# Groups taken from both ends of an image, and three weight chunks loaded ahead, in a two-layer metaformer kernel

## The reference

```python
x = x + deform_conv(ln(x))                      # layer 0: deformable 3x3 convolution
t = tokens(x)                                   # a pixel is a token of 128 numbers
t = t + top2_of_8_experts(ln(t))                # softmax router, 2 of 8 experts per token
x = image(t)
x = x + real(ifft2(mix(fft2(ln(x)))))           # layer 1: spectral mixing by alphas, betas
t = tokens(x)
t = t + top8_tokens_of_64_experts(ln(t))        # each expert takes its best 8 tokens of an image
x = image(t)
```

## Time and profile before

| | us |
|---|---|
| median of 3 runs (4090.9 to 4093.28) | 4091.42 |
| the profiled execution | 4085.3 |
| its span on the core | 4083.4 |
| busy: PE, DVE, ACT, POOL | 3799.8, 2587.2, 1809.6, 1597.7 |
| mean granted TensorE clock, share of full | 0.958 |

### The profile page before, as it was taken

The page is one execution under the profiler, slowest core; times in us unless marked ns, Lnnn a source line. Parts: engine busy times, 40 slices in busy tenths (PEclk is TensorE's granted clock), DMA queues, the critical chain, the costliest instruction groups (busy, mean ns, idle before and its releaser), DMA issues. The chain is left out here.

```text
span 4083.4 us, 88599 instructions
## 1 busy us (share of the span) xinstructions
PE 3799.8 (93%) x31447; PEld 2475.3 (61%) x31447; DVE 2587.2 (63%) x8511; ACT 1809.6 (44%) x4685; POOL 1597.7 (39%) x2857
## 2 busy tenths in 40 slices
PE   7999999999999999999968999999999999986458
PEld 5666666666666666666644445665666656654245
DVE  4444444444444444444428888999999999976633
ACT  4555555555555555555511112444444444456124
POOL 5454544555454544545412222323333233344210
PEclk9999999999999999999979999999999999989755
DMA  5454454554554545444426667777777777744879
GB/s 118 93 100 93 90 93 94 99 94 90 93 94 99 95 89 92 90 91 91 77 68 255 251 250 272 264 278 270 269 271 265 279 262 277 260 154 127 335 275 396
DMA packets 611531, 709.81 MB, mean 174 GB/s; under 512 B 62112, under 2 KB 494112, under 8 KB 594704
## 3 DMA queue, kind: packets, MB, share of 16 engines
q1 hardware_dynamic: 505616, 630.17, 53.7%
q10 hardware_dynamic: 104448, 71.85, 5.8%
q0 software_dynamic: 1024, 2.10, 0.1%
HBM read 521.20 MB, written 181.63 MB: 172 GB/s over the span
## 5 line engine op out<-in xcount | busy, mean ns | idle before, releaser
L362 PE MATMUL a_ob<-a_sr,wcv 128*128 128x512 f32 (+3 forms) x2820 | 1082.1, 518 | 0.8 <-DVE a_xo L492 0.8
L432 ACT COPY a_sr<-a_sb 128x576 f32<-128x576 f32 (+7 forms) x1296 | 621.9, 562 | 900.5 <-PE a_sb L347 892.9
L347 PEld LDWEIGHTS a_sb<-a_tt,a_win 32*128 32x128 f32 x19008 | 659.2, 186 | 258.4 <-issue 242.8
L347 PE MATMUL a_sb<-a_tt,a_win 32*128 32x144 f32 x19008 | 752.2, 301 | 12.8 <-ACT a_sr L432 11.5
L517 POOL TENSOR_TENSOR a_sx<-a_hh 128x576 f32<-128x576 f32 x260 | 378.3, 1455 | 925.5 <-DVE a_hh L469 917.4
L362 PEld LDWEIGHTS a_ob<-a_sr,wcv 128*128 128x128 f32 x2820 | 491.6, 191 | 279.0 <-issue 231.2
L1087 DVE TENSOR_TENSOR b_P<-b_P,b_x 128x1024 f32<-128x1024 f32 x512 | 620.3, 1212 | 0.0
L469 DVE TENSOR_SCALAR a_hh<-a_hh 128x576 f32<-128x576 f32 (+1 forms) x128 | 59.5, 465 | 839.2 <-ACT a_hh L411 839.2
L1217 POOL TENSOR_TENSOR b_ss<-b_st 128x12 f32<-128x12 f32 (+2 forms) x167 | 35.5, 213 | 1094.0 <-DVE b_pp L1162 957.5
L990 PE MATMUL b_z<-b_P,b_ew 128*128 128x512 f32 x1024 | 461.2, 593 | 0.0
L993 PE MATMUL b_z<-b_P,b_ew 128*128 128x512 f32 x1024 | 460.3, 592 | 0.0
(11 more groups left out here) (182 smaller groups left out, 5283.3 us busy)
## 6 DMA issues: line engine op xcount, KB each, us to landing
b_P<-pd SPq DMA_DIRECT2D x128, 2048.0 KB, 7.5
a_win<-xtp SPq DMA_DIRECT2D x2144, 36.0 KB
a_xin<-in_x SPq DMA_DIRECT2D x128, 256.0 KB, 6.0
xtp<-a_tn ACTq DMA_DIRECT2D x128, 256.0 KB, 2.3
x1d<-a_xo SPq DMA_DIRECT2D x128, 256.0 KB, 5.6
b_x<-x1d SPq DMA_DIRECT2D x128, 256.0 KB, 7.4
x2d<-b_xa SPq DMA_DIRECT2D x128, 256.0 KB, 2.7
d_wb<-in_w SPq DMA_DIRECT2D x16, 2048.0 KB, 18.6
```

The lines of the kernel that those rows point to most:

```text
L347: t = e.matmul(d[:, 0:3 * m_, :, NU_ * i:NU_ * i + NU_], win[32 * q:32 * q + 32, half_of(Q, j) % NWH, NWIN // 3 * h + i, :], m, start=(j = ...
L362: t = e.matmul(ob[:, r:r + m, :], k["wcv"][:, 3 * (2 - kr) + kx, :], rows[:, :, t_, :], start=(t_ == 0 and r == 0), stop=(t_ == 8))
L432: a = e.copy(bass.AP(d.tensor, d.offset, [list(d.ap[0]), [1152, ni], [1536, nk], [32, 4], [1, m]]), bass.AP(v.tensor, v.offset, [list(v.ap ...
```

## The change

Three things change.

1. **The order of groups.** Step n of the b half takes group `group_b(n)`: 0, 31, 1, 30, 2, 29, ... within each image. Step n of the c half takes `group_c(n)`: 31, 0, 30, 1, ..., at each step the mirror image of what the b half took at step n. So the c half of step n needs only step n's own mirrored group, and neighbours of `x2d` that were stored at steps n-1 and n+1. `LAG` falls from 39 to 11 and the ring `b_xf` from 35 units to 10. The list ends 28 slots earlier.
2. **The bias matmul** of the expert sum, with the wait for `b_pb`, comes after the eight expert matmuls instead of before them.
3. **Weights ahead.** The memory freed holds a tile `pw` of three chunks, which lives on into phase DE. In slots 118 to 129 SP issues one quarter of a chunk (512 KB) per slot, at the end of the slot. The ring of weights now has 8 slots, 3 in `pw` and 5 in `d_wb`; phase DE issues chunks 3 to 15. The buffers `e_x` and `e_o` lie in `pw`, whose last use by weights is long over when they are first filled.

```diff
-LAG = GI + 7
-XU = 3
-NU = GI + XU
+LAG = 11
+NU = 10
...
+NCH, EC, NW, AHEAD = 8, 8, 8, 3
+def chunk_part(pw, ins, i, part):
+    m, c = CHUNKS[i]
+    n = EC // 4
+    t = pw[:, i * 4096 + part * 1024:i * 4096 + part * 1024 + 1024].rearrange("p (e h) -> p e h", e=n)
+    return t, chunk_source(ins, m, c * EC + part * n, n)
...
 def order_b():
...
+        if 0 <= s - NG + 10 < 4 * AHEAD:
+            out.append(("ahead", s - NG + 10))
...
+def group_b(n):
+    b, i = divmod(n, GI)
+    return b * GI + (GI - 1 - i // 2 if i % 2 else i // 2)
+def group_c(n):
+    b, i = divmod(n, GI)
+    return b * GI + (i // 2 if i % 2 else GI - 1 - i // 2)
+def place_b(g):
+    b, h = divmod(g, GI)
+    return b * GI + (2 * h if h < GI // 2 else 2 * (GI - 1 - h) + 1)
...
             elif stage == "experts":
...
-                w.wait_ge(pb_in[G % NPC], 16 * (G // NPC + 1))
-                e.matmul(ZE[u][:, :, :], ebm[:, :], pb[:, G % NPC, :], start=True, stop=False)
                 for x in range(4):
-                    e.matmul(ZE[u][:, :, :], ew[:, x, :], P[:, G % NPB, :, x, :], start=False, stop=False)
+                    e.matmul(ZE[u][:, :, :], ew[:, x, :], P[:, G % NPB, :, x, :], start=(x == 0), stop=False)
             elif stage == "experts2":
                 for x in range(4, 8):
-                    t = e.matmul(ZE[u][:, :, :], ew[:, x, :], P[:, G % NPB, :, x, :], start=False, stop=(x == 7))
-                t.then_inc(mixed, 1)
+                    e.matmul(ZE[u][:, :, :], ew[:, x, :], P[:, G % NPB, :, x, :], start=False, stop=False)
+                w.wait_ge(pb_in[G % NPC], 16 * (G // NPC + 1))
+                e.matmul(ZE[u][:, :, :], ebm[:, :], pb[:, G % NPC, :], start=False, stop=True).then_inc(mixed, 1)
...
             elif stage == "fourier":
-                w.wait_ge(placed, G // GI * GI + GI)
+                w.wait_ge(placed, G + 1)
...
             elif stage == "load2":
-                g = G + 1 if G % GI < GI - 1 else G + 1 - GI
-                w.wait_ge(x2_out[G % 3], 16 * (G // 3 + 1))
-                w.wait_ge(x2_out[g % 3], 16 * (g // 3 + 1))
+                g = group_c(G)
+                for n in (place_b(g), place_b(g + 1 if g % GI < GI - 1 else g + 1 - GI)):
+                    w.wait_ge(x2_out[n % 3], 16 * (n // 3 + 1))
...
+            elif stage == "ahead":
+                dst, src = chunk_part(k["pw"], ins, G // 4, G % 4)
+                e.dma_start(dst, src).then_inc(k["w_in"][G // 4], 16)
...
-    wb = S("d_wb", [128, NW, 4096])
+    wb = S("d_wb", [128, NW - AHEAD, 4096])
...
-        for i, (m, c) in enumerate(chunks):
+        for i in range(AHEAD, len(CHUNKS)):
+            m, c = CHUNKS[i]
             if i >= NW:
-                used, last = chunks[i - NW]
+                used, last = CHUNKS[i - NW]
                 w.wait_ge(hidden if used == 1 else project, 2 * last + 2)
```

More of the change, by code:

```diff
@@ L844, with chunk_view, chunk_source @@
 NS = NG + LAG
+NCH, EC, NW, AHEAD = 8, 8, 8, 3
+CHUNKS = [(1, 0)]
+for _c in range(1, NCH):
+    CHUNKS += [(1, _c), (2, _c - 1)]
+CHUNKS.append((2, NCH - 1))
+def chunk_view(t, m):
+    return t.rearrange("p (e h) -> p e h", e=EC) if m == 1 else t.rearrange("p (e c o) -> p e c o", e=EC, c=4)
+def chunk_source(ins, m, e0, n):
+    if m == 1:
+        return ins["w1"][e0:e0 + n, 0:128, :].rearrange("e d h -> d e h")
+    return ins["w2"][e0:e0 + n, 0:512, :].rearrange("e (p c) o -> p e (c o)", c=4)
+def chunk_part(pw, ins, i, part):
[3 more added lines that the diff above has]
+    return t, chunk_source(ins, m, c * EC + part * n, n)
 def order_b():
@@ L853, in order_b @@
                 out.append((stage, s - lag))
-    return out
[L857 to L867, removed]
+        if 0 <= s - NG + 10 < 4 * AHEAD:
+            out.append(("ahead", s - NG + 10))
+    return out
+def group_b(n):
[7 more added lines that the diff above has]
+    return b * GI + (2 * h if h < GI // 2 else 2 * (GI - 1 - h) + 1)
 def image_rows(d, G):
-    return d[G * 512:G * 512 + 512, :].rearrange("(r w) c -> w r c", w=128)
+    g = group_b(G)
+    return d[g * 512:g * 512 + 512, :].rearrange("(r w) c -> w r c", w=128)
 def shifted_rows(G):
-    h = G % GI
+    h = group_c(G) % GI
     if h < GI - 1:
@@ L1001, in tensor @@
             elif stage == "fourier":
-                w.wait_ge(placed, G // GI * GI + GI)
+                w.wait_ge(placed, G + 1)
                 w.wait_ge(x3_ready, G)
                 for r in range(4):
-                    t = e.matmul(ZC[:, r, :], xf[:, unit[source(G)], 3 - r, :], al[:, :], start=True, stop=True)
+                    t = e.matmul(ZC[:, r, :], xf[:, G % NU, 3 - r, :], al[:, :], start=True, stop=True)
                 t.then_inc(filtered, 1)
@@ L1050, in scalar @@
                 w.wait_ge(x2_ready, G + 1)
-                w.wait_ge(filtered, freed_by[G])
-                e.copy(xf[:, unit[G], :, 0:1], xn[:, u, :, 0:1])
-                e.copy(xf[:, unit[G], :, 127:0:-1], xn[:, u, :, 1:128]).then_inc(placed, 1)
+                w.wait_ge(filtered, G + 1 - NU)
+                e.copy(xf[:, G % NU, :, 0:1], xn[:, u, :, 0:1])
+                e.copy(xf[:, G % NU, :, 127:0:-1], xn[:, u, :, 1:128]).then_inc(placed, 1)
             elif stage == "norm3":
@@ L1071, in scalar @@
             elif stage == "sums":
-                b, h = divmod(G, GI)
+                b, h = divmod(group_c(G), GI)
                 w.wait_ge(top_ready, G + 1)
@@ L1245, in sync @@
             if stage == "load":
-                b, h = divmod(G, GI)
+                b, h = divmod(group_b(G), GI)
                 w.wait_ge(x2_ready, G + 1 - NX1)
@@ L1337, in phase_de @@
     b1_in, const_in, io_in = sem("b1_in"), sem("const_in"), sem("io_in")
-    w_in = [sem(f"w_in{i}") for i in range(NW)]
+    w_in = k["w_in"]
     got = [sem(f"got{i}") for i in range(8)]
@@ L1358, in phase_de, with ring @@
     POOLS = 11
[L1361 to L1365, removed]
+    place = {c: i for i, c in enumerate(CHUNKS)}
+    def ring(i):
+        i %= NW
+        return k["pw"][:, i * 4096:i * 4096 + 4096] if i < AHEAD else wb[:, i - AHEAD, :]
     def w1(c):
-        return wb[:, place[1, c] % NW, :].rearrange("p (e h) -> p e h", e=EC)
+        return chunk_view(ring(place[1, c]), 1)
     def w2(c):
-        return wb[:, place[2, c] % NW, :].rearrange("p (e c o) -> p e c o", e=EC, c=4)
+        return chunk_view(ring(place[2, c]), 2)
     def w_ready(w, c):
-        w.wait_ge(w_in[place[c] % NW], 16 * (place[c] // NW + 1))
+        i = place[c]
+        w.wait_ge(w_in[i % NW], 16 * (i // NW + 1) + (48 if i % NW < AHEAD else 0))
     def tensor(e):
@@ L1695, in program @@
         k |= {"cv": S("cv", [128, B // 2, 16 * GI]), "ci": S("ci", [128, B // 2, 16 * GI], U32),
-              "cs": S("cs", [128, B // 2, 2 * GI])}
+              "cs": S("cs", [128, B // 2, 2 * GI]), "pw": S("pw", [128, AHEAD * 4096]),
+              "w_in": [ctx.enter_context(nc.semaphore(f"d_w_in{i}")) for i in range(NW)]}
         with ExitStack() as c2:
```

21 lines of the change are left out of this document (8 added, 13 removed).

## The result

| | before | after |
|---|---|---|
| median (lowest to highest) of the runs, us | 4091.16 (4088.93 to 4093.28) | 4000.71 (3995.56 to 4002.66, 4 runs) |
| ratio, 95% interval | 1 | 0.9777 [0.976, 0.9794] |
| profiled execution, its span, us | 4085.3, 4083.4 | 4000.32, 3998.4 |

The changed kernel is 90.4 us faster. A second set of 5 runs gave 4001.2 us, ratio 0.9782 [0.9769, 0.9795].

A forecast was written before the change was run, and what follows sets the result against it. Phase BC was taken as bound by DVE's pace in full slots, DVE waiting for POOL in the head and a round trip in the tail. -101.3 + 33.9 - 8 + 1 - 2 - 5 = -81.4, giving 4010 us, range 4003 to 4032.

The forecast's parts named there:

- The 28 slots: Tail of phase BC, c half alone: slots 139 to 166 go, -101.3 us.
- The six slots behind the last sum: Tail slots 132 to 138: same work as before, so still 31.9 us, no gain.
- The range's low end: Whole kernel: sum with every bound taken, 4007, less 4 for run-to-run and chip difference: 4003 us.
- R2: Tail: the clock stays low until the final drain, four slots at 5.3 instead of 3.6 us, +7, 4017 us; chance 0.08.
- The head and the bias matmul: Phase BC: 28 head slots become full ones, +33.9 us; moving the matmul takes full slots from 11.88 to 11.80, -8.
- R1: Full slots stay at 11.88 us and phase DE gains nothing, 4024 us; chance 0.22 in whole or half.
- The order on SP's queue: Loads of `x2d` rows behind neighbours' stores: cost 0, covered by margins of slots.
- R3: SP stalls at the `x2d` load, delaying `b_P`; 1 us a slot gives 4127 us, slower than before; chance 0.03.
- Weights ahead: Twelve 512 KB loads, one a slot, fit the free DMA time and `b_P`'s 4.4 us slack: +1 us.
- R4: Loads ahead delay the b half by the whole 1.5 us in 12 slots, +17, 4027 us; chance 0.06.
- The start: Phase DE up to the first expert matmul: fewer chunks in flight beside the gathers, -2 us.
- The weights' term: Phase DE, second-layer matmuls: the last weights chunk lands one chunk sooner, -5 us, bounds 0 and -5.1.

The follow-up runs named there:

- again: The kernel before, unchanged, run once more for a second profile: 4091.5 us.
- bias moved: The kernel before with only the bias matmul and its wait moved behind the eight expert matmuls: 4080.32 us, ratio 0.9975.
- order alone: The changed kernel with the bias matmul in front as before, no weights loaded ahead and a weights' ring of 7: 4020.55 us, ratio 0.9832.
- bias first: The changed kernel with the bias matmul and its wait put back in front of the expert matmuls: 4006.97 us, ratio 0.9806.
- not ahead: The changed kernel with the weights' ring of 8 kept but all chunks issued in phase DE: 4000.43 us.
- ahead twice: The changed kernel with each quarter chunk loaded twice, the last one once (11 loads more): 4012.8 us, ratio 0.981.
- lag 25: The changed kernel with nothing loaded ahead, and a lag of 25 and ring of 24 units in place of 11 and 10: 4036.44 us.

## Why the prediction was right and wrong

**The 28 slots.** Right. They took 101.3 us at the end and are gone; a lag of 25 gave back half of them at the same price.

**The six slots behind the last sum.** This is the step that failed most: "The six slots after the b half's last sum (132 to 138) hold the same work as before", priced at the 31.9 us of one profile. The work is the same, the time is not. Ten profiles of kernels that hold these six slots have, in us:

| c half alone for 28 more slots | short tail |
|---|---|
| 31.9 (before), 29.3 (again), 28.9 (bias moved) | 25.3, 26.0 (after), 26.0 (order alone), 27.6 (bias first), 29.5 (not ahead), 29.4 (ahead twice), 27.7 (lag 25) |

What differs between them is how long PE's clock stays at one half (PE's busy time, clock, DMA share, GB/s; the changed kernel, its repeat, the repeat of before, and the first profile of before):

```profile
3654.00:3658.00 4.00, 1.74 (x9) 1.00 0.63 174
3658.00:3662.00 4.00, 2.28 (x15) 1.00 0.36 98
```
```profile
3654.00:3658.00 4.00, 1.60 (x10) 1.00 0.50 138
3658.00:3662.00 4.00, 3.23 (x15) 0.57 0.22 64
3662.00:3666.00 4.00, 2.88 (x18) 1.00 0.48 131
```
```profile
3636.00:3640.00 4.00, 1.58 (x9) 1.00 0.53 147
3640.00:3644.00 4.00, 3.23 (x16) 0.57 0.22 65
3644.00:3648.00 4.00, 3.44 (x13) 0.50 0.41 118
...
3652.00:3656.00 4.00, 3.23 (x17) 0.73 0.15 46
```
```profile
3624.00:3628.00 4.00, 1.59 (x9) 0.94 0.51 140
3628.00:3632.00 4.00, 3.27 (x14) 0.50 0.21 59
...
3644.00:3648.00 4.00, 3.86 (x14) 0.50 0.48 131
```

The same gap in PE's work (1.6 to 1.7 of 4 us busy) is followed by no fall, by one stretch of 4 us at 0.57, by three to four at about one half, or by five, the longest seen. Read so from all ten profiles, the clock was at one half for about 0 us (six slots in 25.3), 3 (26.0, 26.0), 7 (27.6, 27.7), 14 (28.9, 29.3, 29.4, 29.5) and 20 us (31.9): the time of the six slots follows it without exception, by about 0.3 us for each us at one half. The range's low end was built from the bounds of three other terms and "less 4" for chance; the rival R2 counted the clock only as a loss, though the stretch showed the clock at half, so that a full one would bring 31.9 - 25.3 = 6.6 us, to 4003 even with all else as forecast. Two profiles each make this step -4.9 us; the means of the two columns, 30.0 and 27.4, would make it -2.7, so some of the -4.9 may be the luck of the two pairs. Whether the long lag makes the fall longer, or chance alone gave before the high values, stays open: the bias matmul's place does not decide it (26.0 with it in front, 28.9 with it behind), and the two columns overlap.

**The head and the bias matmul.** Right in mechanism, smaller in cost. With the bias matmul still in front the 127 slots grow by 30.2 us (order alone and bias first against before's mean), not 33.9. This is the second term that was mis-sized. Full slots take 11.79 us but for a few longer ones, and the 11.88 was their mean. 28 slots at 11.79 - 10.67 = 1.12 make 31.4, and what the longer slots add up to did not grow with the number of full ones: the move of the matmul takes 9.1 us off the 127 slots in the kernel before, and 7.2 in the changed one, which has 28 full slots more (from the same mean of two). With the fill, 1 us more, the matmul's term is right, -8. R1 (4024 us) is refuted: full slots are at 11.79 and DVE's rate is the limit, as the earlier trace rows had it (11.80). The two terms and the loads come to +21.7 where 26.9 were forecast.

**The order on SP's queue.** Right: cost 0. R3 didn't happen, not even with one slot between store and load (one stall of 4 us, without effect).

**Weights ahead.** Forecast +1, measured 0: the slots with the loads take 11.79 us like the others (`b_xn` at 3476.88, 3488.68, 3500.47, 3512.26, 3524.05 and 3535.84), and R4 is refuted. The Trainium skill, "DMA: Bandwidth & Descriptors", section Bandwidth, from which +7 would have come for DMAs under 1 MiB, is not borne out at one load a slot. At two the cost is +12, by the small store `pd` that comes late behind them; that path, through SP, was not in the term, which reckoned with the DMA engines' free time and `b_P` alone.

**Phase DE.** The start is right (-2.2 for -2), and by the way foretold: the last gather takes 2.55 us in place of 5.28, and with nothing loaded ahead 5.16. The weights' term was sized from the last chunk alone, 5.1 us; all of PE's waits for weights in the stage go from 6.9 to 1.2, and the stretch shrinks by 5.6 to 8 us. Part of the time came from here: -6.8 for -5.

Together: -4.9 from the six slots, -5.2 from head and fill, -1.8 from the weights, -0.2 from the start, and +2.9 from phase A, the drain and the last stage, 9.2 us in all.

## What to carry to other kernels

Each slot of lag in a software pipeline splits one full slot (11.79 us here) into a head slot (10.67) and a tail slot (3.62); what a slot less brings is the difference, here 2.5 us. Price the full slot by its usual time, not by a mean over stalls. A stretch whose time depends on a clock that fell is a term with two ends, and one profile shows only one of them: take its time at full clock as the other bound, or a second profile. Sum all waits for a resource in a stage, not only the last one, before sizing what one more buffer brings.

## What the runs showed of the hardware

- The same work of PE, with the same gap in it (1.6 to 1.7 of 4 us busy), was followed by a granted clock of 1.00 (2.4 GHz), or of 0.50 (1.2 GHz) for up to 20 us. The Trainium skill, "TensorE: Matmul & The Clock Gate", part 1, has activity decide; no measure of activity in the rows above tells the cases apart.
- A 32 KB store that another load waits for lands in 2.5 us with no 512 KB load a slot ahead of it, in 5.2 with one and in 8.3 with two, while the 2 MB load that follows it keeps its 7.2 to 7.6 us. Size alone does not sort them: of two stores of 256 KB, `x2d`, issued nearer behind the added loads, goes from 3.1 to 6.2 and 10.0 us, and `x3d`, issued after both, stays at 2.5 with one load and takes 6.3 with two.
- The same phase A took from 2105.5 to 2115.4 us in the profiles of this study. Of two single profiles, 10 us may be that.
